# Layer 1 of a graph network on one core: the last tile becomes the last gathered one, and ten other tiles are the dense ones

## The reference

```python
loops = jnp.arange(n); src = concat([src, loops]); dst = concat([dst, loops])
deg = jax.ops.segment_sum(ones, dst, n); dinv = rsqrt(deg)
h = x                                              # 6250 x 256
for W, b in ((W1, b1), (W2, b2), (W3, b3)):        # 256x512, 512x512, 512x256
    msg = (h @ W)[src] * (dinv[src] * dinv[dst])[:, None]
    h = relu(segment_sum(msg, dst, n) + b)
out = layernorm(x + h)
```

## Time and profile before

| what | value |
|---|---|
| median of 3 runs | 2491.73 us (2488.53 to 2491.84) |
| profiled execution: its time | 2493.09 us |
| its span, first to last instruction | 2491.3 us |
| mean granted TensorE clock | 0.966 |
| PE busy | 2270.4 us, 91% of the span |
| POOL busy | 1753.5 us, 70% |
| DVE, ACT busy | 1026.0 us (41%), 521.7 us (21%) |
| chain that ended last | PE 61%, POOL 14%, issue 11%, DMA 7% |

### The profile page before, as it was taken

The page is one execution under the profiler, slowest core; times in us unless marked ns, Lnnn a source line. Parts: engine busy times, 40 slices in busy tenths (PEclk is TensorE's granted clock), DMA queues, the critical chain, the costliest instruction groups (busy, mean ns, idle before and its releaser), DMA issues.

```text
span 2491.3 us, 42459 instructions
## 1 busy us (share of the span) xinstructions
PE 2270.4 (91%) x13351; PEld 1563.5 (63%) x13352; DVE 1026.0 (41%) x1307; ACT 521.7 (21%) x1322; POOL 1753.5 (70%) x1837
## 2 busy tenths in 40 slices
PE   6967799999999998899899999999998799999998
PEld 6855577677777773444444444444444688888887
DVE  8878333333333313444444444444423233333332
ACT  6601222222222212222222222222211000000000
POOL 5177777777777757777777777777776776777664
PEclk9788899999999999999999999999999899999999
DMA  6335666666666657888888888888887788888774
GB/s 215 118 116 171 225 204 207 201 199 201 197 204 200 208 169 207 256 269 265 264 267 264 263 266 267 261 264 264 266 267 229 256 254 250 256 248 251 244 245 146
DMA packets 231550, 568.24 MB, mean 228 GB/s; under 512 B 39868, under 2 KB 95795, under 8 KB 231475
## 3 DMA queue, kind: packets, MB, share of 16 engines
q0 software_dynamic: 126752, 399.62, 53.8%
q1 hardware_dynamic: 88371, 126.81, 14.7%
q10 hardware_dynamic: 16352, 40.77, 4.9%
HBM read 476.69 MB, written 90.36 MB: 228 GB/s over the span
## 4 chain that ended last, share of the span: by engine, by line
PE 61%; POOL 14%; issue 11%; DMA 7%; POOLq 3%; DVE 2%; ACT 0%; ACTq 0%; SPq 0%; DVEq 0%
POOL rows L674 14%; PE ps_acc L1514 9%; PE ps_h L1603 8%; PE ps_acc L1518 8%; PE ps_T L1603 7%; PE ps_o L1570 7%; DMA rows<-table,idx 6%; PE ps_d L1615 6%; PE ps_d L1518 5%; PE ps_h L1558 3%; PE ps_d L1514 3%; PE ps_d L1472 2%; POOLq L683 2%; PE ps_e L1591 1%; PE ps_l L1591 1%
## 5 line engine op out<-in xcount | busy, mean ns | idle before, releaser
L674 POOL DMA_INDIRECT rows<-table,idx x912 | 871.0, 955 | 301.3 <-issue 266.2
L674 POOL DMA_INDIRECT rows<-table_parts,idx x884 | 836.2, 946 | 327.6 <-issue 266.3
L895 DVE SCALAR_TENSOR_TENSOR sel<-ps_e,firsts,dstT 128x1152 f32<-128x1152 f32 (+1 forms) x222 | 314.6, 1417 | 685.2 <-PE ps_acc L1514 257.5
L1518 PE MATMUL ps_acc<-rows,sel 128*128 128x512 f32 (+2 forms) x1122 | 487.5, 566 | 87.1 <-DMA rows<-table,idx 65.7
L1518 PE MATMUL ps_d<-rows,sel 128*128 128x512 f32 (+1 forms) x850 | 409.7, 610 | 42.6 <-DMA rows<-table,idx 42.4
L1514 PE MATMUL ps_acc<-rows,sel 128*128 128x256 bf16 (+1 forms) x2196 | 361.6, 281 | 48.9 <-DMA rows<-table_parts,idx 21.1
L1518 PEld LDWEIGHTS ps_acc<-rows,sel 128*128 128x128 f32 x1122 | 207.9, 201 | 253.0 <-issue 160.8
L1514 PEld LDWEIGHTS ps_acc<-rows,sel 128*128 128x128 bf16 x2196 | 218.5, 100 | 93.5 <-issue 36.6
L1518 PEld LDWEIGHTS ps_d<-rows,sel 128*128 128x128 f32 x850 | 151.6, 194 | 195.0 <-issue 138.8
L1570 PE MATMUL ps_o<-w,hT 128*128 128x512 f32 (+1 forms) x784 | 270.5, 488 | 1.2 <-ACT hT L1275 1.2
L1615 PE MATMUL ps_d<-parts,made_tiles 128*128 128x256 bf16 x1470 | 229.2, 272 | 0.2 <-issue 0.2
(11 more groups left out here) (190 smaller groups left out, 1904.8 us busy)
## 6 DMA issues: line engine op xcount, KB each, us to landing
built<-made_tiles SPq DMA_DIRECT2D x72, 384.0 KB, 4.7
made_tiles<-built ACTq DMA_DIRECT2D x72, 384.0 KB, 4.5
rows<-table,idx POOLq DMA_INDIRECT x912
rows<-table_parts,idx POOLq DMA_INDIRECT x884
table<-made SPq DMA_DIRECT2D x49, 256.0 KB
acc<-table SPq DMA_DIRECT2D x49, 256.0 KB
built<-made_tiles SPq DMA_DIRECT2D x24, 416.0 KB, 4.8
made_tiles<-built ACTq DMA_DIRECT2D x24, 416.0 KB, 5.0
```

What stands on the lines that cost most here:

```text
L674: pool.indirect_dma_start(out=to, out_offset=None, in_=its[0:nodes, :], in_offset=bass.IndirectOffsetOnAxis(ap=idx[:, of, k:k + 1], axis=0 ...
L895: v.scalar_tensor_tensor(to[:, k:k + FRONT, :], numbers.unsqueeze(1).broadcast_to([P, FRONT, P]), firsts[:, bass.ds(t, 1)], dstT[:, bass.d ...
L1518: return mm(to[:, 0:w], sel[:, k, :], rows_of[phase][:, k, 0:w] if first is None else first, start=start, stop=stop)
```

## The change

Tile 48 is now the last *gathered* tile of layer 1: the last window (place T-1 of the flow) is for tile 48 instead of tile 38. The ten dense tiles are 38 to 47 instead of 39 to 48. The 49 dense steps of the last macro are all done in its first two windows (18 in b = 0, 31 in b = 1, `LAST_CUTS`), so that the last dense tile, 47, is complete before the last window begins; its flow (now place T-2) runs inside the last window, behind that of tile 37 (place T-3), whose own places move forward to (2, 4, 7). After the last window only tile 48 is left to pass the flow.

With the tiles, other things move. The block of tile 48 is now built first in layer 2 instead of in layer 1 (`place_of`), for layer 3; the last window of layer 1 gathers its slot 0 afresh; and `own_rows` of the last window fetches tile 48's rows. Tile 48 has the edges 98,320 to 99,999, so its `need` is 13 and its slots 16 and 17 are skipped; tile 38's is 16. GpSimd's last two windows of layer 1 and SP's first six windows of layer 2 are written out instead of looped. GpSimd's wait at the head of layer 2 is as before.

```diff
+        def tile_of_dense(k):
+            return GATHER_1 - 1 + k
+        def flow_of_last():
+            return T - 2
...
         def place_of(q, layer_1):
-            return q + DENSE - DENSE_1 if layer_1 else q - DENSE_1
+            if layer_1:
+                return q + DENSE - DENSE_1 - 1
+            return DENSE - 1 if isinstance(q, int) and q == DENSE_1 else q - DENSE_1 - 1
...
-                    def rows_and_store(t, s, *pieces):
+                    def rows_and_store(t, s, *pieces, n=None):
+                        before = t - 1 if n is None else n - 1
-                        own_rows(t)
+                        own_rows(t, n)
...
-                        store(t - 1, s)
+                        store(before, s)
...
+                            elif isinstance(m, int) and m == DENSE_1 - 1 and b == PER - 1:
+                                rows_and_store(T - 1, flow_in(m, b), n=t)
...
-                        store(GATHER_1 - 1, T - 2)
+                        store(tile_of_dense(DENSE_1 - 1), flow_of_last())
                         store(T - 1, T - 1)
...
-                        with pool.Fori(MACRO // 2 + 1, GATHER_1 // 2) as i:
+                        with pool.Fori(MACRO // 2 + 1, GATHER_1 // 2 - 1) as i:
                             two(i)
+                        t = GATHER_1 - 2
+                        need = pool.value_load(need_i[0:1, t:t + 1], min_val=0, max_val=99)
+                        window(0, t, t % 2, need, in_parts=True)
+                        need = pool.value_load(need_i[0:1, T - 1:T], min_val=0, max_val=99)
+                        window(0, GATHER_1 - 1, (GATHER_1 - 1) % 2, need, in_parts=True, afresh=True)
...
-                        else:
+                        elif build:
                             tile(0, t, t, s, 1, half)
+                        else:
+                            scale(0, t, t, s, 1)
+                            scale_dense(m, s + 1)
+                            keep_aggT(s, aggT[:, 0:C], 0)
+                            relus(s)
+                            keep_aggT(s + 1, aggT_1, C)
+                            make(0, t, s)
+                            relus(s + 1)
+                            make(0, tile_of_dense(m), s + 1)
...
-                scale(0, GATHER_1 - 1, GATHER_1 - 1, T - 2, 1)
-                scale_dense(DENSE_1 - 1)
-                keep_aggT(T - 2, aggT[:, 0:C], 0)
-                relus(T - 2)
-                make(0, GATHER_1 - 1, T - 2)
-                keep_aggT(T - 1, aggT_1, C)
+                scale(0, T - 1, GATHER_1 - 1, T - 1, 1)
+                keep_aggT(T - 1, aggT[:, 0:C], 0)
                 relus(T - 1)
                 make(0, T - 1, T - 1)
...
-                DENSE_CUTS = [0, 11, 29, T]
+                DENSE_CUTS, LAST_CUTS = [0, 11, 29, T], [0, 18, T, T]
...
-                        lo_h, hi_h = DENSE_CUTS[b:b + 2]
+                        lo_h, hi_h = (DENSE_CUTS if builds else LAST_CUTS)[b:b + 2]
+                        final = not builds and b == PER - 1
-                        places = (7, 10, 13) if b == 1 and not first else PLACES[0]
+                        places = (2, 4, 7) if final else (7, 10, 13) if b == 1 and not first else PLACES[0]
...
+                            if final and at == 5:
+                                turn(0, s + 1, agg_1, C)
+                            if final and at == 8:
+                                hidden(s + 1, aggT_1)
+                            if final and at == 12:
+                                product(0, s + 1)
...
-                turn(0, T - 2)
-                hidden(T - 2)
-                turn(0, T - 1, agg_1, C)
-                product(0, T - 2)
-                hidden(T - 1, aggT_1)
+                turn(0, T - 1)
+                hidden(T - 1)
                 product(0, T - 1)
```

More of the change, by code:

```diff
@@ L483, in phases, with own_rows @@
                         sp.wait_ge(stored, 16 * T * phase)
-                    def own_rows(t):
-                        n = nth(phase, t) if per > 1 else nth_of_windows(phase, t)
+                    def own_rows(t, n=None):
+                        if n is None:
+                            n = nth(phase, t) if per > 1 else nth_of_windows(phase, t)
                         sp.wait_ge(acc_used, n + 1)
@@ L554, in macro @@
                                 store_built(*pieces)
-                                store(GATHER_1 + m - 1, flow_of_dense(m - 1))
+                                store(tile_of_dense(m - 1), flow_of_dense(m - 1))
                                 store(t - 1, flow_in(m, b))
                                 store_built(*pieces[0:3], pieces[3] + 1)
+                            elif isinstance(m, int) and m == DENSE_1 - 1 and b == PER - 1:
+                                rows_and_store(T - 1, flow_in(m, b), n=t)
                             else:
@@ L593, in three @@
                                 store_parts(t - 2)
-                        with sp.Fori(0, SIXES) as i:
+                        for u in range(2):
+                            three(0, u)
+                        with sp.Fori(1, SIXES) as i:
                             for u in range(2):
@@ L1059, in one_window, with steady @@
             def one_window():
-                def steady(phase, t, odd, hots=None, whole=None, units=None, last=False, in_parts=False):
+                def steady(phase, t, odd, hots=None, whole=None, units=None, last=False, in_parts=False, tile=None, next_tile=None):
                     n = nth_of_windows(phase, t)
+                    t, next_tile = t if tile is None else tile, t + 1 if next_tile is None else next_tile
                     base = base_of(t)
-                    next_base = None if last else base_of(t + 1)
+                    next_base = None if last else base_of(next_tile)
                     prepare(n, t, base, 0, sel_parts if in_parts or phase == 2 else sel)
@@ L1114, in macro @@
                         steady(0, MACRO + PER * m + b, (MACRO + PER * odd + b) % 2, hots,
-                               (m, place_of(m, True), of) if b == 0 else None, last=not build and b == PER - 1, in_parts=True)
+                               (m, place_of(m, True), of) if b == 0 else None, last=not build and b == PER - 1, in_parts=True,
+                               tile=T - 1 if not build and b == PER - 1 else None,
+                               next_tile=T - 1 if not build and b == PER - 2 else None)
                 macro(0, 0, 0)
@@ L1265, in scale, with scale_dense @@
                 act.sem_inc(acc_used, 1)
-            def scale_dense(k):
+            def scale_dense(k, s):
                 act.wait_ge(dense_1_done, k + 1)
                 act.sem_inc(act_step, 1)
-                nc.scalar.activation(agg_1, ps_dense_1, ACT.Copy, scale=dinv[:, bass.ds(GATHER_1 + k, 1)]).then_inc(agg_ready, 1)
-                act.wait_ge(agg_ready, flow_of_dense(k) + 1)
+                nc.scalar.activation(agg_1, ps_dense_1, ACT.Copy, scale=dinv[:, bass.ds(tile_of_dense(k), 1)]).then_inc(agg_ready, 1)
+                act.wait_ge(agg_ready, s + 1)
                 act.sem_inc(dense_1_free, 1)
@@ L1365, in macro @@
                             scale(0, t, t, s, 1)
-                            scale_dense(m - 1)
+                            scale_dense(m - 1, flow_of_dense(m - 1))
                             keep_aggT(s, aggT[:, 0:C], 0)
@@ L1375, in macro @@
                                 keep_pairs(*half, range(0, 2))
-                            make(0, GATHER_1 + m - 1, flow_of_dense(m - 1))
+                            make(0, tile_of_dense(m - 1), flow_of_dense(m - 1))
                             if half is not None:
@@ L1383, in macro @@
                             make(0, t, s)
-                        else:
-                            tile(0, t, t, s, 1, half)
+                        elif build:
+                            tile(0, t, t, s, 1, half)
+                        else:
+                            scale(0, t, t, s, 1)
[6 more added lines that the diff above has]
+                            make(0, tile_of_dense(m), s + 1)
                 first_macro()
@@ L1620, in one_window, with steady @@
             def one_window():
-                def steady(phase, t, places, beside=None, s=None, ps=None, in_parts=False, afresh=False):
+                def steady(phase, t, places, beside=None, s=None, ps=None, in_parts=False, afresh=False, tile=None):
                     n = nth_of_windows(phase, t)
@@ L1624, in steady @@
                         s = nth(phase, t - 1)
-                    need = pe.value_load(need_i[0:1, bass.ds(t, 1)], min_val=0, max_val=99)
+                    need = pe.value_load(need_i[0:1, bass.ds(t if tile is None else tile, 1)], min_val=0, max_val=99)
                     if afresh:
@@ L1703, in beside @@
                                 dense_1(m, of, range(lo_h + (at - start) * n // wide, lo_h + (at - start + 1) * n // wide))
```

(3 more changed lines are left out.)

## The result

The changed kernel takes 2483.62 us (median of 9 runs, 2481.14 to 2488.14) against 2491.84 us for the one before beside it (9 runs, 2488.53 to 2492.28). The ratio is 0.9974, with a 95% interval of 0.9966 to 0.9982, which is 4.5 to 8.5 us, and by itself 6.5; the medians as such lie 8.2 us apart. The forecast, -6.0 us, lies inside the interval. The span of the profiled execution is 2482.9 us with a mean granted clock of 0.968.

A forecast was written before the change was run, and what follows sets the result against it. POOL, issuing without pause, was taken to bound layer 2, so its restart counts: window 6.55 us later, `made` of T-2 at x = 16.03, store 2.99, thus 6.16 us sooner; taken as -6.0, forecast 2485.7 us, range 2482.3 to 2490.0.

The forecast's parts named there:

- POOL sets layer 2: Layer 2: POOL issues gathers every 1.25 us without a break, so its start time sets when the layer ends.
- The restart, 6.16 us sooner: End of layer 1: POOL's first gather of layer 2 moves from 938.88 to 932.72.
- dense steps: Last macro: twenty steps of 0.3276 us move ahead of the last window, which starts 6.55 us later.
- the layout of the window: Last window of layer 1: product of T-2 ends at x = 15.21, `made` at 16.03, POOL's gather at 19.02.
- the store: Head of layer 2: 2.99 us from the end of `made` of T-2 to POOL's first gather.
- One term: Tail of layer 1 before the change: hidden of 3.59 us at granted clock 0.56, a stretch that leaves T-2's path.
- SyncE: Last window: `own_rows` issued at x = 10.9, tile 37's store 0.4 later, freeing `made` at 14.6, 0.7 us to spare.
- PE's own end: End of layer 1: PE free at 940.0 against 942.4, only 2.4 us sooner, its lateness gone by slot 3.
- PE holding layer 2 back: First window of layer 2: only PE's own 2.4 us come through, 2489.3 us; 12% together with a late tile 37 store.
- The wait ending with something else: Head of layer 2: free slots or copied indices end POOL's wait instead; no gain, 2491.7 us; 6%.
- A code gap: Last window: one PE stand of 4.42 us without recorded cause leaves 1.7 of the 6.2 us, 2490.0 us; 6%.
- Half clock in the last window: Last window: 13.3 us of PE work take 26.6, POOL starts 7.2 us later than before, 2498.9 us; 5%.

The follow-up runs named there:

- the kernel before with the longer wait: Kernel before, GpSimd waiting at layer 2's head for all 49 tile stores instead of 48: 2498.07 us, ratio 1.0032.
- the cuts alone: Kernel before with only the last macro's dense steps cut 18, 31, 0: ratio 0.9968 on a chip of 3129 us, 1.0002 on that of 2491.67 us.
- The exchange alone: Changed kernel keeping only the tile exchange, cuts 11, 18, 20, T-2's flow behind the window: against before 0.9975 (3129 us chip), 0.9990 (2491.67 us chip).
- the flows are closer together: Changed kernel, last window's flows closer, tile 37 stored before own rows are fetched: 0.9960 and 0.9954 to before, chips of 3129 us.

## Why the prediction was right, point by point

*POOL sets layer 2.* Right: both profiles have 1552.4 us from the restart to the end (1552.4 to 1553.9 in the five on chips of this speed), and a restart made later lengthens the run by as much (6.2 us of span for 5.85 in the kernel before with the longer wait). On the chips of 3129 us GpSimd isn't without a pause, and the traces there don't show it.

*The restart, 6.16 us sooner.* 6.18 by the two profiles, from a common point. Each term: dense steps, 19.83 us from first slot to first slot in b = 0 instead of 17.54 and 25.09 instead of 20.93 in b = 1, so 6.45 where 6.55 was worked out; the layout of the window, 19.10 against 19.02; the store, 3.00 from the end of `made` against 2.99.

*One term stood on a clock that varies.* The sum took the before side from its profile, with hidden at 3.59 us and a granted clock of 0.56, and asked only whether the last window would keep its clock, not whether that stretch of before was typical. The same tail, with the same waits (1.15 and 1.04 or 1.05 us), stands in four more profiles. From the start of hidden to that of `made` it took 7.88 us before; 7.72 and 7.70 in the two runs of the cuts alone and 7.94 in that of the written-out code, all with a stretch at a low clock (means of 0.54 to 0.81 there); and 6.36 at 1.00 in the kernel before with the longer wait. In the second run of the cuts the clock fell later, so that the hidden has a part and the product the rest:

```profile
927.64 2.75 PE L1558 MATMUL ps_h<-post,w 128*128 128x128 f32 x16 [1.04 <-ACT post L1280]
930.85 4.36 PE L1570 MATMUL ps_o<-w,hT 128*128 128x512 f32 x8
```

With 6.36 the change would gain 4.7 us (6.18 - 1.52), with the mean of the five, 7.52, an estimated 5.8. So most of the stretch belongs to what the change gains, since T-2's flow now lies between slots at 1.00, but its 1.5 us aren't there in every execution. The exchange alone doesn't tell on this: its waits are other ones (0.32 and 0.47 us). The ratio, 6.5 with 4.5 to 8.5, holds both values; the medians, 8.2 us apart, are over them. What is over I can't assign: it is the size of what executions differ by ahead of the last macro.

*SyncE.* Right, 10.9 and then 0.4; `made` of T-2 started 0.13 us behind the product, so the store of tile 37 was in time. When it landed isn't in the rows.

*PE's own end.* Forecast 940.0 and 2.4 us sooner than before; it came at 936.05, 6.2 sooner. 2.3 of the 4 us by which it beat the forecast are the earlier start of the window in this execution, 1.5 the hidden at full clock after it (930.00, 2.05 us). Its lateness did not matter.

*The rivals.* PE holding layer 2 back: no, it waits 3.00 us before slot 3. The wait ending with something else: no, a store ended it. But the prediction had the indices copied before x = 16, and that was wrong:

```profile
928.33 0.17 DVE L906 COPY idx<-srcT 128x18 int32 x1
```

The copy is done at x = 17.1, behind the sum of the last window. With the 0.9 to 1.0 us that lie between this copy and GpSimd's gather where the flows are closer together (1207.88 - 1207.01; 1201.30 - 1200.32), GpSimd could have started at 929.4 to 929.5, 1 us ahead of when the store let it. So the rival's ground was weaker than the prediction says: the copy ended 1.0 us behind `made` of T-2, not before it, and only the 3.00 us of the store hid it.

A code gap: none in the window, though two skips stand there. Half clock in the last window: it was at 1.00 throughout (windows view after the change):

```profile
910.80:928.00 17.20, 16.55 (x100) 11.51 (x100) 3.30 (x5) 5.30 (x14) 3.78 (x4) 1.00 0.39 111
928.00:930.00 2.00, 0.44 (x2) 0.20 (x2) 1.75 (x3) 0.89 (x2) 0.00 (x0) 1.00 0.35 131
930.00:932.10 2.10, 2.05 (x16) 1.86 (x16) 0.00 (x0) 0.01 (x1) 1.31 (x2) 1.00 0.00 0
```

16.55 of 17.20 us busy, and the 2 us of waiting behind it did not bring the clock down this time.

## What to carry to other kernels

Where an engine runs without a pause through a whole stage, look for what it waits for at the stage's head, and take just that off the end of the stage before: here the store of the last tile but one, by moving its flow under other work, 6 us of 2492, passed on whole. Then list every wait that stands at that head with the time at which it ends: here the copy of the indices would have let GpSimd start only 1 us sooner than the store did, and it took some 0.3 us of what the next edit won. Count such an edit from a common point near it in both traces; from the start of the execution a quarter of the difference here (2.2 of 8.4 us) lay ahead of anything that was moved. And take the length of a stretch after a wait from several executions: a stretch at the low clock was worth 1.5 of the 6.2 us, and it stood in four of the five profiles of that tail.

## What the runs showed of the hardware that I had not expected

The granted clock after the same short waits isn't the same in each execution. After 1.15 and 1.04 us without PE work it fell to 0.56 in the kernel before, and with the same instructions and waits of 1.15 and 1.05 us it stayed at 1.00 in the kernel before with the longer wait (hidden 2.05 us). Over all profiles it fell in four of five with these waits. Behind the last window of the changed kernel and its variants, where the waits are 1.15 and 0.47 us, it fell in two of seven (hidden 3.43 and 3.38 us, at 0.56 and 0.57; 2.05 in the others). The Trainium skill ("TensorE: Matmul & The Clock Gate", The HAM clock gate) calls the activity window of the clock's monitor free-running, and says that one and the same kernel therefore has different numbers of matmuls at the low clock after its start. It says this of a kernel's start; these traces show such a difference behind short waits.

One kernel took 2491.67 us on one chip and 3123 to 3129 us on three others, with instructions of the same length, and ScalarE standing in one piece with no releaser on the core, for 9.6 us before a `made` and 11.8 us before an `hT`. There, work put into PE's holes was free (10 us faster with the cuts alone); on the other chip the same edit gained nothing. What made the engines stand there isn't known from these traces.
